# The output gate taken out of the first product group of an LSTM that runs beside a leaky cell

## The reference, cut to what matters

```python
# layer 0: leaky cell, then a mixture of 8 experts added to x (top 1)
state = leak * state + gate(x_t, state) ...        # L0_cond2
x = x + L0_ffn(L0_cond2(...))
# layer 1: LSTM over that x
z = xz_t + prev_h @ Wh;  i, f, o = sigmoid(z[:3]);  g = tanh(z[3])
next_c = f * prev_c + i * g
next_h = o * tanh(next_c)
```

## Time and profile before

| | us |
|---|---|
| median of three runs (4470.17 to 4472.15) | 4471.25 |
| the profiled execution, its own time | 4479.49 |
| its span, first to last instruction | 4477.7 |
| granted TensorE clock, mean over the span | 0.971 |
| TensorE busy, weight loads | 4172.4, 2953.7 |
| VectorE busy, ScalarE busy | 2397.2, 1957.7 |
| products of zeros (L761), 932 in the program | 285.6 |

### The profile page before, as it was taken

The page is one execution under the profiler, slowest core; times in us unless marked ns, Lnnn a source line. Parts: engine busy times, 40 slices in busy tenths (PEclk is TensorE's granted clock), DMA queues, the critical chain, the costliest instruction groups (busy, mean ns, idle before and its releaser), DMA issues. The chain is left out here.

```text
span 4477.7 us, 117287 instructions
## 1 busy us (share of the span) xinstructions
PE 4172.4 (93%) x41024; PEld 2953.7 (66%) x41024; DVE 2397.2 (54%) x7200; ACT 1957.7 (44%) x5039; POOL 772.5 (17%) x3244
## 2 busy tenths in 40 slices
PE   6998999999999899999899999999999797889999
PEld 4555777777776455555455787787877455556666
DVE  5775654555554577777355444666666553431111
ACT  4333443333332566666233222665656452333333
POOL 1111221000000366665122000111111210000000
PEclk9999999999999999999899998999999997989999
DMA  1000000000000000000000000000000100000000
GB/s 55 0 0 26 1 0 10 17 0 0 0 0 10 1 2 2 1 1 1 35 0 0 4 0 0 2 3 3 3 3 3 54 0 1 0 1 5 4 5 7
DMA packets 4097, 29.03 MB, mean 6 GB/s; under 512 B 432, under 2 KB 944, under 8 KB 2352
## 3 DMA queue, kind: packets, MB, share of 16 engines
q1 hardware_dynamic: 3776, 24.97, 1.4%
HBM read 22.87 MB, written 2.10 MB: 6 GB/s over the span
## 5 line engine op out<-in xcount | busy, mean ns | idle before, releaser
L604 DVE TENSOR_REDUCE cells_row_max<-banks 128x4 f32<-128x512 f32 x384 | 238.5, 683 | 163.8 <-PE banks L397 163.8
L2604 ACT ACTIVATE experts_hidden<-banks,weights 128x512 f32<-128x512 f32 x256 | 175.8, 687 | 262.9 <-PE banks L2546 261.3
L761 PE MATMUL banks<-clock_fill 128*128 128x512 bf16 x932 | 285.6, 395 | 1.2 <-PEq L101 1.2
L2554 PEld LDWEIGHTS banks<-weights,experts_hidden 128*128 128x128 f32 x2048 | 238.6, 192 | 30.1 <-issue 30.1
L2546 PE MATMUL banks<-act_a,weights 128*128 (+1 forms) x512 | 244.8, 609 | 11.3 <-PEq L101 10.6
L2624 DVE SCALAR_TENSOR_TENSOR experts_acc<-banks,experts_gate,experts_acc 128x128 f32<-128x128 f32 x224 | 63.1, 344 | 348.3 <-PE banks L2554 348.3
L541 ACT ACTIVATE cells_probs<-banks 128x512 f32<-128x512 f32 x384 | 198.3, 602 | 95.5 <-PE banks L437 90.0
L2554 PE MATMUL banks<-weights,experts_hidden 128*128 128x128 f32 x2048 | 238.8, 274 | 0.0
L604 DVE TENSOR_REDUCE attn_row_max<-banks 128x4 f32<-128x512 f32 x256 | 158.9, 683 | 134.6 <-PE banks L397 134.6
L2822 ACT ACTIVATE lin_context_turned<-banks 128x256 f32<-128x256 f32 x128 | 49.2, 384 | 403.9 <-PE banks L2774 403.9
L1578 ACT ACTIVATE wave_hidden_turned<-banks,weights 128x128 f32<-128x128 f32 x512 | 205.9, 455 | 16.5 <-PE banks L1522 13.3
(11 more groups left out here) (539 smaller groups left out, 10156.6 us busy)
## 6 DMA issues: line engine op xcount, KB each, us to landing
weights<-in_p SPq DMA_DIRECT2D x1, 2894.5 KB, 15.9
weights<-in_p SPq DMA_DIRECT2D x1, 2894.0 KB, 9.3
weights<-in_p SPq DMA_DIRECT2D x2, 1396.0 KB, 7.2
x_res<-in_x SPq DMA_DIRECT2D x1, 2048.0 KB, 15.1
out_x<-x_res SPq DMA_DIRECT2D x8, 256.0 KB, 2.0
weights<-in_p SPq DMA_DIRECT2D x1, 1836.0 KB, 11.3
weights<-in_p SPq DMA_DIRECT2D x1, 1835.5 KB, 7.0
weights<-in_p SPq DMA_DIRECT2D x1, 1344.5 KB, 9.9
```

The lines of the kernel that those rows point to most:

```text
L604: dve.tensor_reduce(mt[:, 4 * g:4 * g + 4], bank, AX_X, ALU.max).then_inc(s["max_ready"], 1)
L761: pe.matmul(core.ps[:, bank, :], core.fill[:, 0:P], core.fill[:, :], start=True, stop=True)
L2554: last = pe.matmul(ps[:, OUT + e % 2, t * P:(t + 1) * P], hs[:, e % 2 * DEPTH + f, t * P:(t + 1) * P], w("W2", (e * DEPTH + f) * P, P), st ...
L2604: act.activation(hs[:, e % 2 * DEPTH + f, :], ps[:, f % 2, :], ACT.Gelu, bias=w("b1", j, 1)).then_inc(s["h_ready"], 1)
```

## The change

The gates are laid out in PSUM in the order i, f, g, o in place of i, f, o, g (`GATES`). The product of o is no longer in the first group: PE does three gates (z_done), the leaky product, and then the product of o, which waits until ACT has read the bank for the three gates (th_ready), and raises o_done. ACT does the tanh of three gates, the leaky gate, the tanh of o, the tanh of the cell. DVE makes the output gate after the leaky gate. The two waits before h change places. The leaky product is made 128 columns wide in place of 32, by repeating the state four times, into three places that nobody reads. `FILLS` becomes 0, 1, 1, 1. The copies that pick the bias of each gate become nine in place of three.

```diff
-    FILLS = (2, 3, 2, 3)
+    FILLS = (0, 1, 1, 1)
+    GATES = (0, 1, 3, 2)
...
             def leaky(st):
                 past(pe, s["leaky_ready"], st.s())
                 lo = st.c % 4 * NB
-                pe.matmul(ps[:, 2 + st.c // 4 % 2, lo:lo + NB].unsqueeze(1), w("WhT"), leaky_state(st), start=False,
+                out = ps[:, 2 + st.c // 4 % 2, :].rearrange("p (j t) -> p j t", j=4)
+                pe.matmul(out[:, :, lo:lo + NB], w("WhT"), leaky_state(st).broadcast_to([P, 4, NB]), start=False,
                           stop=True, skip_group_check=True).then_inc(s["leaky_z_done"], 1)
-            def lstm(st):
+            def lstm(st, part):
                 past(pe, s["h_ready"], st.s(-FIRST_LAG))
                 state = const("cond").unsqueeze(1) if st.c == FIRST_LAG else positions(core.a, st.s(-FIRST_LAG - 1))
-                for z in range(4):
-                    lo = (z * AHEAD + st.c % 4) * NB
+                if part == 1:
+                    pe.wait_ge(s["th_ready"], st.s(1 - FIRST_LAG))
+                for at, z in list(enumerate(GATES))[3 * part:3 + part]:
+                    lo = (at * AHEAD + st.c % 4) * NB
                     last = pe.matmul(ps[:, st.c // 4 % 2, lo:lo + NB].unsqueeze(1), v("Wh", z * P, P), state,
                                      start=False, stop=True, skip_group_check=True)
-                last.then_inc(s["z_done"], 1)
+                last.then_inc(s["o_done" if part else "z_done"], 1)
...
             def body(st, known):
                 if lstm_runs(st, known):
-                    lstm(st)
+                    lstm(st, 0)
                 if leaky_runs(st, known):
                     leaky(st)
+                if lstm_runs(st, known):
+                    lstm(st, 1)
...
-            def lstm_tanh(st):
+            def lstm_tanh(st, part):
                 act.wait_ge(s["z_done"], st.s(1 - FIRST_LAG))
+                if part == 0:
+                    act.activation(th[:, 0:3, :], here[:, 0:3, :], ACT.Tanh).then_inc(s["th_ready"], 1)
+                    return
+                act.wait_ge(s["o_done"], st.s(1 - FIRST_LAG))
+                act.activation(th[:, 3:4, :], here[:, 3:4, :], ACT.Tanh).then_inc(s["to_ready"], 1)
...
                 if st.c == 6:
                     for base in (0, 32, 64):
+                        for lo, hi, z in ((0, 2, 0), (2, 3, 3), (3, 4, 2)):
+                            dve.tensor_copy(pick[base:base + 4, lo:hi, :, :], gate[:, z:z + hi - lo].broadcast_to(
+                                [4, hi - lo, AHEAD, NB])).then_inc(s["bias_ready"], 1)
...
-                dve.tensor_scalar(og[:, :], th[:, 2, :], 0.5, 0.5, ALU.mult, ALU.add).then_inc(s["gate_ready"], 1)
+            def output_gate(st):
+                dve.wait_ge(s["to_ready"], st.s(1 - FIRST_LAG))
+                dve.tensor_scalar(og[:, :], th[:, 3, :], 0.5, 0.5, ALU.mult, ALU.add).then_inc(s["gate_ready"], 1)
             def state(st):
+                dve.wait_ge(s["tc_ready"], st.s(1 - FIRST_LAG))
                 dve.wait_ge(s["gate_ready"], st.s(1 - FIRST_LAG))
-                dve.wait_ge(s["tc_ready"], st.s(1 - FIRST_LAG))
...
                 if leaky_runs(st, known):
                     leaky_gate(st)
                 if lstm:
+                    output_gate(st)
                     state(st)
```

More of the change, by code:

```diff
@@ L838, in leaky_experts_lstm_stage @@
             "hot_ready", "unit_ready", "masked_ready", "turn_done", "gelu_ready", "gt_ready", "out_done", "stored",
-            "z_done", "th_ready", "parts", "c_ready", "gate_ready", "tc_ready", "h_ready", "const_ready"]}
+            "z_done", "o_done", "th_ready", "to_ready", "parts", "c_ready", "gate_ready", "tc_ready", "h_ready", "const_ready"]}
         block = ctx.enter_context(nc.Block())
@@ L929, in lstm_pre @@
                         pe.wait_ge(s["halved"], 3)
-                        pe.wait_ge(s["bias_ready"], 4)
+                        pe.wait_ge(s["bias_ready"], 10)
                     pe.matmul(ps[:, bank, :], bias_w[0:68, :], pick[0:68, :, :, :], start=True, stop=False,
@@ L933, in lstm_pre @@
                 out = ps[:, bank, k * AHEAD * NB:(k + 1) * AHEAD * NB].rearrange("p (t b) -> p t b", t=AHEAD)
-                pe.matmul(out, v("Wx", k * P, P), positions(core.x, st.s(4 - k - FIRST_LAG), AHEAD), start=False,
+                pe.matmul(out, v("Wx", GATES[k] * P, P), positions(core.x, st.s(4 - k - FIRST_LAG), AHEAD), start=False,
                           stop=False, skip_group_check=True)
@@ L1008, in _ @@
             act.wait_ge(s["leak_ready"], 2)
-            def lstm_tanh(st):
+            def lstm_tanh(st, part):
                 act.wait_ge(s["z_done"], st.s(1 - FIRST_LAG))
-                act.activation(th[:, :, :], ps[:, st.c // 4 % 2, :].rearrange(
-                    "p (g t b) -> p g t b", g=4, t=AHEAD)[:, :, st.c % 4, :], ACT.Tanh).then_inc(s["th_ready"], 1)
+                here = ps[:, st.c // 4 % 2, :].rearrange("p (g t b) -> p g t b", g=4, t=AHEAD)[:, :, st.c % 4, :]
+                if part == 0:
[3 more added lines that the diff above has]
+                act.activation(th[:, 3:4, :], here[:, 3:4, :], ACT.Tanh).then_inc(s["to_ready"], 1)
             def leaky_tanh(st):
@@ L1044, in body @@
                 if lstm_runs(st, known):
-                    lstm_tanh(st)
+                    lstm_tanh(st, 0)
                 if leaky_runs(st, known):
                     leaky_tanh(st)
+                if lstm_runs(st, known):
+                    lstm_tanh(st, 1)
                 if lstm_runs(st, known):
@@ L1098, in prepare @@
                     for base in (0, 32, 64):
-                        dve.tensor_copy(pick[base:base + 4, :, :, :], const("gate_pick", rows=4).rearrange(
-                            "p (g b) -> p g b", g=4).unsqueeze(2).broadcast_to([4, 4, AHEAD, NB])).then_inc(
-                            s["bias_ready"], 1)
+                        gate = const("gate_pick", rows=4).rearrange("p (g b) -> p g b", g=4).unsqueeze(2)
+                        for lo, hi, z in ((0, 2, 0), (2, 3, 3), (3, 4, 2)):
+                            dve.tensor_copy(pick[base:base + 4, lo:hi, :, :], gate[:, z:z + hi - lo].broadcast_to(
+                                [4, hi - lo, AHEAD, NB])).then_inc(s["bias_ready"], 1)
                 if st.c == 10:
@@ L1123, in cell @@
                                          op1=ALU.mult).then_inc(s["parts"], 1)
-                dve.scalar_tensor_tensor(out=ic[:, :], in0=th[:, 0, :], scalar=1.0, in1=th[:, 3, :], op0=ALU.add,
+                dve.scalar_tensor_tensor(out=ic[:, :], in0=th[:, 0, :], scalar=1.0, in1=th[:, 2, :], op0=ALU.add,
                                          op1=ALU.mult).then_inc(s["parts"], 1)
```

## The result

4567.45 us median (4539.65 to 4573.66) against 4471.7 us before (4470.17 to 4474.2): ratio 1.0202, 95% interval 1.016 to 1.0243. The forecast was 4466.6, the range ended at 4492.

The account below looks back on a forecast made before the run. Loop steps were taken as bound by the dependency chain, or by TensorE's queue in the hidden and output steps. Loop -9.4, written-out 0.0, LSTM alone +4.8, leaky -0.1 sum to -4.7: 4466.6 us, 8-in-10 range 4453 to 4492.

Parts of the forecast that it names:

- third rival: Shared stage: with fewer zeros the granted clock falls to half; representative time 4490 us, chance 0.20.
- three such steps: Shared-stage loop steps at half clock, +1.7 us each: three cancel the gain, ten give +12, a third of the loop +50.
- output step: Loop step with the expert's output product: TensorE's queue sets it, 2.74 us after the change against 2.76 before.
- the wide leaky product gives back at most 8 records: Shared stage: against 1.5 us less streaming of zeros in four steps, the wider product returns up to 8 records, 0.11 each.
- The ring: Loop step's dependency chain from weight load through tanh, o's product, output gate and h to the next load: 2.64 us against 2.75.
- second rival: Loop: the new handshake costs what it saves, o's load taking 0.22 instead of 0.05; 4483 us, chance 0.15.
- hidden step: Loop step with the expert's hidden product: TensorE's queue sets it, 2.73 us after the change against 2.86 before.
- first rival: Loop: TensorE's queue doesn't bind, so all steps go at 2.64 us; 4458 us, chance 0.20.
- fourth step: Loop step with c mod 4 = 3: less to do on TensorE, so it stays with the dependency chain at 2.64 us.
- Written-out shared steps: 12 steps before the loop and 4 after: four take 10.74 us against 10.76, a change of 0.0.
- LSTM alone: Steps after the shared stage: four zeros queue behind o's late product, plain step 2.79 against 2.57; +4.8 us in all.
- leaky part: 16 steps of the leaky cell alone: wide product +1.0, copies +0.3, fewer clock dips -1.4, together -0.1 us.

Follow-up runs that it names:

- e2: Kernel before the change with only the products of zeros cut from ten to three in four steps, narrow leaky product: 4592.8 us.
- e13: Changed kernel with 104 memsets moving VectorE's loop code (no stall), three zeros in four steps, leaky product narrow again: 4612.8 us.
- e14: Kernel before the change with three zeros in four steps and the leaky product made wide: 4487.0 us.
- e5: Changed kernel with 104 memsets ahead of the loop that only move VectorE's code, no stall: 4526.7 us, runs 4469 to 4577.
- e6: Changed kernel with the old ten zeros in four steps and 104 memsets moving VectorE's code, no stall: 4498.6 us.
- e7: Changed kernel with one product of zeros per shared step in the gap before o's product, and 104 memsets moving VectorE's code: 4468.7 us.
- e4: Changed kernel with one product of zeros per shared step in the gap before o's product, VectorE's stall still there: 4544.9 us.
- e9: As e7, but each LSTM-alone step has one product of zeros in the gap and three behind it instead of four behind: 4464.7 us.
- e3: Kernel before the change with only the two waits ahead of h swapped: 4468.6 us.
- e11: As e3, with one product of zeros fewer in steps with c mod 4 = 0 (nine in four steps): 4456.6 us.
- e8: Kernel before the change with only six one-column memsets added to VectorE's program ahead of the stage: 4501.0 us.
- e1: Changed kernel with the old ten products of zeros in four steps, VectorE's stall still there: 4514.5 us.

## Why the prediction was wrong

**The step that failed** is the clock. The sum has no term for it: the forecast takes it as 1.00 in the stage, as in the earlier trace rows. Only the third rival, "The clock falls in the shared stage", has it, at 0.20 and a price of 4490; its cause was named rightly and its size was not. With "three such steps", "ten", "a third of the loop +50" I priced dips like those of the earlier trace rows, 3.4 us long. Measured: 304 us at half clock, with 63 of the 96 loop steps wholly in it, and the loop +92.6. No step cost more than the +1.7 that I had, but there were far more of them: they took 4.41, 3.64, 4.39 and 3.60 us for 2.745, 2.666, 2.745 and 2.732 (1.61, 1.37, 1.60 and 1.32 times; "about 1.6" held for the hidden and the output step). With the narrow product a few zeros too few are not a few dips: in e2 and e13 the clock, once down, stayed down for 440 and 451 us, with TensorE busy 60.00 and 59.98 of 60 us in the rows; the forecast took each dip for one that ends by itself. And "the wide leaky product gives back at most 8 records" undervalued it: it is the difference between e14 and e2. The clock alone is enough for the miss: without the stall at the branch the median is still 4526.7, and seven of ten runs lie at 4492 or more (e5).

**What the prediction did not have** is the branch. It counted the six more copies as time (+0.3) and not as code. By e6 the five stalls and the dips behind them cost the changed order 16 us with the old zeros, by e7 and e4 76 us with few: the stall takes down a clock that would otherwise have held.

**Point by point, at full clock.**
- The ring (forecast in brackets). The load of o's product starts 0.05 after the tanh's end (0.05), ACT 0.09 after the product (0.09), tanh 0.250 and 0.197 (0.25, 0.20), h 0.20 after the output gate (0.20). Steps of c mod 4 = 1 take 2.666 (2.64). Right. So the second rival, the handshake, is out.
- The hidden step, 2.745 (2.73). Right: TensorE's weight loads leave 0.04 us free before the next LSTM product. So the first rival, that the queue doesn't bind, is out for this step.
- The output step, 2.745 (2.74). The number is right by luck, the mechanism is not: the queue leaves 0.22 us free there. VectorE sets the step, since the expert's routing runs past the tanh's end: fc starts 0.21 after it where it takes 0.03 elsewhere. In e7, whose step is as long, with the tanh's end at 601.99:

```profile
602.20 0.19 DVE L1143 SCALAR_TENSOR_TENSOR first_fc<-first_gates_tanh,first_c_twice 128x32 f32<-128x32 f32 x1
603.58 0.75 PEld L927 LDWEIGHTS banks<-act_a,weights 128*128 128x128 f32 x6 [0.22 <-issue]
```

- The fourth step (c mod 4 = 3), 2.732 (2.64). TensorE has 0.40 us free before the next product, so the queue is not it: in this step alone o's load starts 0.11 after the tanh's end and not 0.05, and that is the difference to 2.666. It is as late as in the written-out steps (0.11, forecast 0.13); why in this step of the loop, no run shows. Four steps are 10.89 for 10.75, the gain 24 x 0.24 = 5.7 for 9.4.
- Written-out shared steps 2.805 and 2.561 (2.81, 2.56). Right, 0.0.
- LSTM alone: 36.5 at full clock (e5, e6) against 32.05 before, +4.4 in twelve steps (+4.8 in all). Right, and e9 shows the cause.
- The leaky part: -3.3 (-0.1). Both early dips of the earlier trace rows are gone, but they are gone in e3 as well, which has the narrow product, and the runs of one kernel before spread over 18 us. Not shown to be the change's.

At full clock the change would have been worth about nothing, -5.7 + 4.8: the three fastest runs of e5, with a mean clock of 0.973 to 0.974, take 4469 to 4470, 4 to 5 us under the 4474.2 beside them.

**By stretch**, the profiled runs: -3.3 before the first tanh, 0 written out, +92.6 loop, +5.4 steps 124 to 127, +8.7 LSTM alone, -1.4 the last three, in all +102. The stages behind are untouched and took 7.8 less than in the profiled run of before, which lay 8 us over its median.

**What stays open:** why, with three zeros and the wide product, the clock of e5 falls in some executions, and of the changed kernel at 465.2 us, ahead of any branch; and which of the fetched blocks the branch misses.

## What to carry to other kernels

Products of zeros are no slack: before taking some away, look at every real product that has to stand in for them, and don't price the clock by single dips: it can stay down for the whole stage (e2, e13). Put what must stay into a gap where the engine waits anyway, where they cost nothing (e7), and take them away one by one (e11). Instructions ahead of a loop are part of the loop's cost: compare each engine's time over its back edge, and its instruction fetches, before and after. Of a change in several parts try each part alone: here two swapped lines in the old order (e3, loop 262.5) give as much as the whole new order at its best (e9, 262.1). And check each step's own mechanism, not only its time: the output step's time was as forecast for another reason.

## What the hardware showed that I had not expected

- A branch back over 321 recorded VectorE instructions costs 0.3 or 3.4 us, depending on six instructions ahead of the loop (e8 against before).
- In a stage at full clock, stalls of TensorE of 1.9 to 2.4 us were each followed by 3.4 to 23.9 us at the lower level where ten zeros stand in four steps (e1, e8), and in the loop the clock never fell where the stall was gone (e6, the kernel before).
- In e14 nine dips stand in the stage, eight of them 3.4 us long and one 27.3; seven of the eight distances between their starts are 34.1 us, in steps that repeat every 11 us.
